# Host-turned weights, a later routing prefix and later result-buffer waits in a convolution and expert kernel

## What is computed

```python
out = x
for i, typ in enumerate(('same', 'upsample', 'same', 'downsample')):
    s = style @ mod_w[i].T + mod_b[i]                  # style: 128 x 64
    weight = SCALE * w[i] * s[:, None, :, None]        # w: 32 x 32 x 3 taps
    weight = weight * rsqrt(sum(weight ** 2) + eps)    # per sample and output channel
    out = conv(out, weight, typ) + b[i]                # with a blur where it resamples
h = out.reshape(4096, 512)
scores = sigmoid(h @ gate_w.T) + bias                  # 16 experts
topk_w, topk_idx = top_k(scores, 4); topk_w /= sum(topk_w)
z = silu(h @ Wg[e].T) * (h @ Wu[e].T)                  # per expert, 256 wide
y = sum over the four experts of topk_w * z @ Wd[e].T
y = y + (silu(h @ Sg.T) * (h @ Su.T)) @ Sd.T           # the shared expert
return x + y
```

## Time and profile before

| | us |
|---|---|
| median of 3 runs | 1312.61 (1310.80 to 1313.75) |
| the profiled execution | 1313.15 |
| its span, first to last instruction | 1311.4 |
| first group's layers to the last group | about 40 to 570 |
| jobs | 591.0 to 1298.6 |
| mean granted clock of PE, share of full | 0.978 |

### The profile page before, as it was taken

The page is one execution under the profiler, slowest core; times in us unless marked ns, Lnnn a source line. Parts: engine busy times, 40 slices in busy tenths (PEclk is TensorE's granted clock), DMA queues, the critical chain, the costliest instruction groups (busy, mean ns, idle before and its releaser), DMA issues. The chain is left out here.

```text
span 1311.4 us, 24385 instructions
## 1 busy us (share of the span) xinstructions
PE 1219.5 (93%) x5979; PEld 975.9 (74%) x5980; DVE 856.5 (65%) x2459; ACT 497.1 (38%) x1087; POOL 564.5 (43%) x844
## 2 busy tenths in 40 slices
PE   5799999999999999839999999999999999999996
PEld 4577777777777777638888788888888888888884
DVE  7588888888888888755555555555555654554553
ACT  3454544445445554413232332323233332322331
POOL 0022222222222222235656556565655556666554
PEclk8799999999999999969999999999999999999998
DMA  4365455444444444326566565666657665656564
GB/s 149 91 170 136 130 130 130 129 129 130 130 130 130 130 129 127 96 92 145 111 146 105 127 122 110 144 108 133 119 97 190 148 143 106 107 111 103 99 105 79
DMA packets 124484, 162.16 MB, mean 124 GB/s; under 512 B 23200, under 2 KB 78496, under 8 KB 124464
## 3 DMA queue, kind: packets, MB, share of 16 engines
q0 software_dynamic: 35616, 74.08, 31.3%
q1 hardware_dynamic: 87552, 87.84, 23.6%
q10 hardware_dynamic: 1296, 0.01, 0.1%
HBM read 73.18 MB, written 55.18 MB: 98 GB/s over the span
## 5 line engine op out<-in xcount | busy, mean ns | idle before, releaser
L398 POOL DMA_INDIRECT lists<-entry,place x128 | 136.4, 1065 | 419.7 <-DVE place L803 388.5
L206 PE MATMUL bank<-wup_hi,xt_hi 128*128 128x512 f32 x680 | 272.3, 400 | 0.8 <-ACT xt_hi L533 0.8
L206 PE MATMUL bank<-wup_lo,xt_hi 128*128 128x512 f32 x680 | 269.9, 397 | 0.0
L430 POOL DMA_INDIRECT out_rows<-yb,sid x140 | 223.7, 1598 | 88.3 <-DVE yb L978 64.3
L416 POOL DMA_INDIRECT xg<-h_rows,gid x140 | 140.6, 1004 | 187.3 <-PE bank L1197 128.8
L213 PE MATMUL bank<-wup_hi,xt_lo 128*128 128x512 f32 x680 | 192.3, 405 | 0.0
L965 DVE TENSOR_TENSOR z<-sg,bank 128x256 f32<-128x256 f32 x138 | 58.2, 422 | 174.0 <-ACT sg L620 174.0
L620 ACT ACTIVATE sg<-bank 128x256 f32<-128x256 f32 x138 | 52.9, 384 | 283.2 <-PE bank L213 283.2
L206 PEld LDWEIGHTS bank<-wup_hi,xt_hi 128*128 128x128 f32 x680 | 129.1, 190 | 30.9 <-issue 1.0
L206 PEld LDWEIGHTS bank<-wup_lo,xt_hi 128*128 128x128 f32 x680 | 128.7, 189 | 29.5
L206 PE MATMUL bank<-x_hi,cwt_hi 128*128 128x512 f32 (+1 forms) x352 | 141.9, 406 | 8.6 <-ACT x_hi L510 3.7
(11 more groups left out here) (209 smaller groups left out, 2034.2 us busy)
## 6 DMA issues: line engine op xcount, KB each, us to landing
x<-x1p SPq DMA_DIRECT2D x256, 64.0 KB
x<-x1p SPq DMA_DIRECT2D x256, 63.8 KB
xraw<-in_x SPq DMA_DIRECT2D x32, 256.0 KB, 2.6
xbase<-in_x SPq DMA_DIRECT2D x32, 256.0 KB
h_rows<-hrow SPq DMA_DIRECT2D x128, 64.0 KB
out_rows<-orow SPq DMA_DIRECT2D x32, 256.0 KB, 2.1
wraw<-in_L_ffn_Wg SPq DMA_DIRECT2D x11, 512.0 KB, 4.8
wraw<-in_L_ffn_Wu SPq DMA_DIRECT2D x11, 512.0 KB, 5.5
```

The source lines that it names most:

```text
L206: r = pe.matmul(dst, lhs[a if data_moves else 0], rhs[0 if data_moves else a], start=n == 0 and a == 0, stop=False)
L398: pool.indirect_dma_start(out=lists, out_offset=bass.IndirectOffsetOnAxis(ap=place[:, par, k:k + 1], axis=0), in_=entry[:, par, k, :], in_ ...
L430: pool.indirect_dma_start(out=out, out_offset=bass.IndirectOffsetOnAxis(ap=sid[:, u, :], axis=0), in_=yb[:, u, :], in_offset=None, compute ...
```

## The change

The host lays out the weights so that the contracted dimension is first: `styleT`, `modT` (already repeated four times), `gateT`, and for each expert one array for up (gate and up halves side by side) and one for down. All transposes of weights on PE are gone, with the banks and waits that they had; ACT and DVE read `wraw` and `wdraw` themselves. Each expert is loaded by two DMAs (1 MB and 512 KB, 8 KB and 4 KB in a piece instead of 2 KB and 1 KB). SP loads the next expert when DVE has written the last low part (`w_lo`). In the first job of an expert the chunks stand one by one between the other steps of ACT and DVE, the last two at the end. In the groups the prefix matmuls stand behind layer 0 of the next group. PE waits for each `yb` ahead of the down projection that leads to it.

```diff
@@ SP
-            sp.dma_start(modw[:], mod_w.rearrange("l c d -> (l c) d")).then_inc(S["style_loaded"], 16)
-            sp.dma_start(sty[:], style).then_inc(S["style_loaded"], 16)
+            sp.dma_start(modwt[:], modT).then_inc(S["style_loaded"], 16)
+            sp.dma_start(styt[:], styleT).then_inc(S["style_loaded"], 16)
...
             def load_expert(number):
-                sp.dma_start(wraw[:, 0:IC, :], Wg[bass.ds(number, 1)].rearrange("a (m p) h -> p (a m) h", p=P)).then_inc(S["raw_loaded"], 16)
-                sp.dma_start(wraw[:, IC:, :], Wu[bass.ds(number, 1)].rearrange("a (m p) h -> p (a m) h", p=P)).then_inc(S["raw_loaded"], 16)
-                sp.dma_start(wdraw[:], Wd[bass.ds(number, 1)].rearrange("a (m p) i -> p (a m) i", p=P)).then_inc(S["raw_loaded"], 16)
+                sp.dma_start(wraw[:], Wup[bass.ds(number, 1)].rearrange("a p c i -> p (a c) i")).then_inc(S["raw_loaded"], 16)
+                sp.dma_start(wdraw[:], Wdn[bass.ds(number, 1)].rearrange("a p c h -> p (a c) h")).then_inc(S["raw_loaded"], 16)
...
             with sp.Fori(0, experts) as i:
-                sp.wait_ge(S["w_t"], (i + 2) * (HC + IC))
+                sp.wait_ge(S["w_lo"], (i + 2) * (HC + IC))
@@ ACT
             def weights_hi(n, b, c):
-                act.wait_ge(S["w_t"], n * (HC + IC) + (c + 1))
-                act.activation(dst, wbank(n, c)[:], ACT.Copy).then_inc(S["w_hi"], 1)
+                raw = wraw[:, c, :] if c < HC else wdraw[:, c - HC, :]
+                if c == 0:
+                    act.wait_ge(S["raw_loaded"], n * 32 + 32)
+                act.activation(dst, raw, ACT.Copy).then_inc(S["w_hi"], 1)
...
-                w(0, 1)
                 gate(0)
-                w(2, 3)
+                w(0)
                 z_in(0)
+                w(1)
                 gate(1)
                 turned_in(j + 1, 0)
-                w(4)
+                w(2)
                 z_in(1)
-                w(5)
+                w(3)
                 turned_in(j + 1, 1)
+                w(4, 5)
@@ DVE
-            dve.wait_ge(S["modt_ready"], 1)
-            dve.tensor_copy(styt[:], bank[6][0:SD, P:2 * P])
-            dve.tensor_copy(modwt[:], bank[6][0:SD, 0:P].rearrange("d (l a c) -> d l a c", l=NL, a=1).broadcast_to([SD, NL, NB, C])).then_inc(S["modt_copied"], 1)
...
+                raw = wraw[:, c, :] if c < HC else wdraw[:, c - HC, :]
...
-                dve.tensor_tensor(dst, wbank(n, c)[:], hi.bitcast(F32), ALU.subtract).then_inc(S["w_lo"], 1)
+                dve.tensor_tensor(dst, raw, hi.bitcast(F32), ALU.subtract).then_inc(S["w_lo"], 1)
...
-                w(0, 1)
                 glu(0)
-                w(2, 3)
+                w(0)
                 z_in(0)
+                w(1)
                 glu(1)
                 turned_in(j + 1, 0)
-                w(4)
+                w(2)
                 z_in(1)
-                w(5)
+                w(3)
                 weighted(0)
                 turned_in(j + 1, 1)
                 weighted(1)
+                w(4, 5)
@@ PE, body
+                if tail < 1:
+                    if not (early and g < 2):
+                        pe.wait_ge(S["logit_ready"], g - 1)
+                    layer0(g + 1)
                 if not (early and g < 2):
                     pe.wait_ge(S["mask_ready"], g - 1)
                     pe.wait_ge(S["zt_lo"], g - 1)
                     pe.matmul(bank[7][:, 0:E], tri[:], mask[:], start=True, stop=False)
                     pe.matmul(bank[7][:, 0:E], ones[:], cum[:, par, :], start=False, stop=True).then_inc(S["prefix_done"], 1)
-                if tail < 1:
-                    if not (early and g < 2):
-                        pe.wait_ge(S["logit_ready"], g - 1)
-                    layer0(g + 1)
...
-                        for c in range(HC + IC):
-                            turn_weights(0, c)
-                        pe.wait_ge(S["w_lo"], HC + IC)
...
-                    if not (early and g == 1):
+                    if early and g == 1:
+                        pe.wait_ge(S["w_lo"], HC + IC)
+                    else:
                         pe.wait_ge(S["z_ready"], g - 1)
@@ PE, job
                 pe.wait_ge(S["b_zt_lo"], j * 2 + 2)
-                w_taken(0)
-                w(0, 1)
+                if ahead is not None:
+                    pe.wait_ge(S["w_lo"], ahead * (HC + IC))
                 pe.wait_ge(S["b_xt_hi"], j * 2 + 1)
...
                 lo_passes(pe, bank[0][:], up(0, b)).then_inc(S["b_up"], 1)
-                pe.wait_ge(S["b_y"], j * 2 + 2)
-                w(2, 3)
-
                 pe.wait_ge(S["b_xt_hi"], j * 2 + 2)
                 hi_passes(pe, bank[1][:], up(1, b))
-                w_taken(1)
...
                 turn_in(j + 1, 0)
-                w(4)
-                w_taken(3)
-
+
+                pe.wait_ge(S["b_y"], j * 2 + 1)
                 pe.wait_ge(S["b_zt_hi"], j * 2 + 1)
                 hi_passes(pe, bank[6][:], down(0, b))
...
                 turn_in(j + 1, 1)
                 lo_passes(pe, bank[6][:], down(0, b)[1:]).then_inc(S["b_down"], 1)
-                w(5)
-                w_taken(4)
+                pe.wait_ge(S["b_y"], j * 2 + 2)
                 pe.wait_ge(S["b_zt_hi"], j * 2 + 2)
                 hi_passes(pe, bank[7][:], down(1, b))
```

More of the change, by code:

```diff
@@ L1022, in _ @@
                 r.then_inc(S["diag_t"], 1)
-            pe.wait_ge(S["gate_loaded"], 16)
-            for c in range(HC):
-                r = pe.transpose(bank[6][:, c * E:(c + 1) * E], gnat[:, c:H:HC], ident[0:E, 0:E])
-            r.then_inc(S["gate_t"], 1)
-            pe.wait_ge(S["modt_copied"], 2)
+            pe.wait_ge(S["wsqt_ready"], 1)
             for l in range(NL):
@@ L1204, in job @@
             def job(j, ahead, b):
-                def w(*chunks):
-                    for c in chunks if ahead is not None else ():
-                        turn_weights(ahead, c)
-                def w_taken(n):
-                    if ahead is not None:
-                        pe.wait_ge(S["w_lo"], ahead * (HC + IC) + n)
                 pe.wait_ge(S["b_zt_lo"], j * 2 + 2)
-                w_taken(0)
-                w(0, 1)
+                if ahead is not None:
+                    pe.wait_ge(S["w_lo"], ahead * (HC + IC))
                 pe.wait_ge(S["b_xt_hi"], j * 2 + 1)
```

90 lines of the change are left out of this document (45 added, 45 removed).

## The result

The changed kernel takes 1292.11 us in the median (1291.28 to 1295.22, four runs) where the kernel before took 1312.86 beside it: a ratio of 0.9849, 95% interval 0.9834 to 0.9863, or about 20 us off. I had forecast 1281.0 with a range from 1273 to 1291. The direction is right, the size is not: a third of the forecast gain of 32.2 us is missing.

A forecast was written before the change was run, and what follows sets the result against it. PE was taken as the bound, busy 1219.5 of 1311.4 us. Gains of 0.7 (start), 5.8 (groups), 4.7 (end of groups, first job) and 21.0 (other first jobs), 32.2 off 1313.15, gave 1281.0 us; 8-in-10 range 1273 to 1291.

The forecast's parts named there:

- Start: Before the groups: DVE loses two copies ahead of the tap chain, worth 0.7 us, bounds 0 and 1.0.
- I take 0: Start of layer 1: lower PE clock after idle time could cost eight matmuls 1.6 us; counted as 0.
- Groups: Prefix matmuls behind layer 0: PE waits for `x0_lo` instead of the mask; 0.20 us a group, 5.8 us in 29.
- the rival that gives nothing: Groups: reordering gains nothing or loses 0.1 us, as DVE's longer queue returns as a late split; 1287 to 1290, chance 0.14.
- the one that wins all 0.88: Groups: the whole 0.88 us mask wait is won, 29 x 0.68 us more, 1261 us; chance 0.03.
- one of my signs of being wrong: Groups: a wait of PE for `x_hi` of layers 2 or 3 in each group would show the forecast wrong.
- End of the groups: Before the jobs: 24 transposes go, DVE's wait for the prefix ends, so the chain to the gathers starts 2.2 us earlier.
- The load of the second expert: Entry into the jobs: SP's load moves behind `w_lo`; its two DMAs have some 10 us until ACT asks; no cost counted.
- First job: First job after the groups: six up matmuls at the low clock cost 1.2 us; it lasts 11.35 us.
- First jobs: Other nine experts: each loses 2.68 us of transposes, gives back 0.35 for a late `z`; 2.33 each, 21.0 us in sum.
- The moved result-buffer waits: Jobs: the moved `b_y` waits have results that are ready in either place, so they cost nothing.
- POOL's issues: Rival in first jobs: subtractions with two SBUF inputs hold up POOL's DMA issues, 23 us over ten jobs, 1304 us; chance 0.04.

## Why the prediction was off, step by step

**Start (-0.7, measured +0.69).** DVE's chain is as much earlier as I said (13.02 for 13.71 at the transposes), but "I take 0" for the clock was wrong: PE's matmuls behind it run at the low level, eight of them taking 2.08 us for 1.16 (in twelve of the thirteen traces with this start), and so do those of layer 0. At layer 1 of group 0 the 0.7 us are used up (39.83 for 39.77). I had priced the risk with 1.6 us and left it out. The other 0.63 us come behind that, where the level changes at other moments in each execution; with starts from 54.95 to 57.62 us in one program they are chance as far as the traces tell.

**Groups (-5.8, measured -5.34; undone, +4.2).** Right in mechanism and size. The wait changes its releaser; neither the rival that gives nothing nor the one that wins all 0.88 came. On the second kind of chip the term is 26.6 us, for a delay that no row before could show, and one of my signs of being wrong stands there: PE waits for `x_hi` in each group (7.6 us in 19 places).

**End of the groups (-2.2, measured -2.88).** The term was right. DVE's mask of the last group and `cum`, before:

```profile
565.91 0.27 DVE L870 TENSOR_REDUCE mask<-hot 128x16 bf16<-128x64 f32 x1
```

and after:

```profile
560.75 0.26 DVE L859 TENSOR_REDUCE mask<-hot 128x16 bf16<-128x64 f32 x1
561.98 0.16 DVE L783 TENSOR_TENSOR cum<-cum,mask 128x16 bf16<-128x16 bf16 x1
```

From the mask to `cum` it was 569.41 - 565.91 = 3.50 us and is 1.23, so 2.27 less. Another 0.5 us were not forecast: the mask itself comes sooner in its group, where more of PE's matmuls run at the upper level (the four passes of the last down projection ahead of `zt_lo` start 0.23 to 0.31 us apart, and 0.42 to 0.57 before).

**The load of the second expert ("have some 10 us until ACT asks for them").** This is the step that failed most. I asked when the load is wanted, not what it meets. It met the second gather, for which PE waited 3.0 us; kept apart, 2.7 of them come back, and 0.5 us at the first gather.

**First job (1.2 us for the low clock).** Too small by 0.6: the first up projection took 5.39 us to its sigmoid, where 1.2 us on top of the old job's 3.63 would be 4.83. I had six matmuls at the low level, and all twelve were. With the working of the old first job (0.7) these are 1.3 us.

**First jobs (12.48 to 10.15, measured 10.40).** The chunk ahead of `z` cost 0.14 us, less than my 0.35, but with the chunk behind it `zt_lo` is 0.36 us late, so the price of the chunks was right in sum. The copy out of SBUF took 0.62 us as estimated. What failed is that I took all of a first job's excess over 9.80 us for weights: about 0.19 of it was the way into the next loop, which stays wherever the chunks stand. Over ten first jobs, and beside the 0.04 us of the next step, I was short by 0.2 each, 2.1 us.

**The moved result-buffer waits ("nothing").** 0.043 us for each of 68 jobs, 2.9 us. The two waits do keep PE from waiting for `yb`, as it would with the old one now that DVE waits more often for the additions. One wait at the first down projection gives jobs of 9.80 us, and 1.2 to 1.6 us of the 2.9 from first to last sigmoid.

**The rivals.** POOL's issues were not held up: `out_rows` issues take 1621 ns in the mean for 1598, `xg` 1022 for 1004. By the rule that the prediction takes from the Trainium skill, "SBUF — State Buffer", "Who interferes with whom", subtractions with two SBUF inputs contend with POOL's reads of SBUF. The same section adds, as inferred, that such an instruction leaves the writing of DMA descriptors alone, and the trace agrees with that, to 1 or 2%. Yet the sign that I had named for this rival, an addition into the output that delays `yb`, did come, by another way: the additions land later, and DVE waits for them for 27.2 us. In this trace PE loses nothing by it. The clock did not fall in the groups: the distance there is still 0.23 us with 0.66 to 0.79 us of idle in each.

What did come was none of my rivals but four things at once, against the terms above: 3.0 us for the load, 2.9 for the waits, 2.1 for first jobs and 1.4 at the start, the last partly by chance. Each stood in the working as nothing or nearly nothing and hardly any could gain, and the range left no room for them: its upper end, 1291, came from the rivals alone. The 0.7 us won at the end of the groups, mostly by the clock, made the miss a little smaller, and that was luck.

## What to carry to other kernels

Take each edit that is costed at "nothing" and ask three things of it: what runs on the DMA engines at the moment to which a transfer is moved, whether a wait costs time at its new place even when it has long been reached, and what clock PE has when its work before a stretch is gone. Where a job is longer than its neighbours, do not put all of the excess to the work that is about to go: a part can be the way from one loop into the next. And where a wait changes its releaser, look whether that operation can stand earlier on its engine: that was worth 9 us on the first kind of chip, where the whole reordering it followed from was worth 4 to 5; on the second kind it was 2.4 us.

## What the runs showed of the hardware

- The same program is slower on some chips: the kernel before takes 1350 to 1352 for 1314.4 us, the changed one 1308.7 for 1293.1. Jobs are equal to 0.01 us; in the groups ACT starts one copy up to 1.9 us later. A change's worth can so double, 42 us for 21.
- A wait for a semaphore that has long been reached costs PE 0.04 us ahead of one matmul and nothing ahead of another (9.84 and 9.80 us).
- From the DVE result that ends its last wait of a first job to the first matmul in the next loop PE takes 1.22 to 1.28 us in six traces, against 1.16 within a loop; to the next sigmoid it is 4.35 against 4.16 us.
- A gather issued together with 1.5 MB of weights took 6.7 us, at 360 GB/s of all DMA; apart it took 3.45, and PE waits 0.28 us for it, not 3.00.
- One program starts differently from execution to execution: the first transposes of `hrow` came at 54.95 to 57.62 us, with a granted clock of 1.00 or 0.50 over the same 4 us.
